# Gate and up products of 16 experts from two scaled fp16 parts in place of two fp32r parts

## The chip, the cores and the metric

The kernel runs on one NeuronCore of a Trainium2 chip (PE the matmul engine, DVE the vector engine, ACT the scalar engine, POOL, and SP for DMAs). The metric is the device time of one execution in microseconds.

## What is computed

A cross attention and then a soft mixture of experts on 16 batches of 100 tokens with 256 features. The expert part, with n tokens, 16 experts e of 64 slots s, and 512 hidden features f:

```python
logits = einsum('bnd,esd->bnes', x, se)
dispatch = softmax(logits, axis=1)
combine = softmax(logits.reshape(B, N, -1), axis=-1)
slots = einsum('bnd,bnes->besd', x, dispatch)
gate = gelu(einsum('besd,edf->besf', slots, Wg) + bg, approximate=False)
up = einsum('besd,edf->besf', slots, Wu) + bu
eout = einsum('besf,efo->beso', gate * up, Wd) + bd
out = x + einsum('bns,bso->bno', combine, eout)
```

Here x in the first line is a layer norm with gain norm_g and bias norm_b. Results are wanted at fp32 quality, so large products are made from a high and a low part of each operand: high x high, high x low and low x high.

## The kernel before

Three phases follow each other, each a block of its own, and at a block's end all engines meet.

**Attention** takes one batch per step of a hand-written table of slots. Its products of probabilities and values (L762) use fp16 probabilities as weights and 49 bf16 columns. In step 15 (B - 1) and the step before, DVE also prepares the first token norm of the next phase.

**Routing** runs steps t from -2 to 17. In step t, PE makes the logits of batch t + 1 (L1167), ACT copies those of batch t to l_sb (L1075), DVE takes maxima, ACT exponentiates (e_comb L1084, e_disp L1103, eight pieces), and for batch t - 1 DVE takes the reciprocal rz_slot (L1012), POOL scales (disp_n L964), PE transposes (L1138, L1152), and ACT and DVE copy the results out (combT L1091, dispT L1018) for SP to store in DRAM. The order on each engine is the order of the calls of `part`, with `part` of slot s + 6 for the batch before ahead of slot s. In routing's last steps, PE also makes the first slots of the expert phase (L1224). Gate and up weights of experts 0 and 1 (wgu) are loaded in steps -1 and 0.

**Experts** run as 8 pairs, `step(pair, first, last)`, of which six are a loop. Each pair has two halves h of the batches (8 batches x 64 slots = 512 columns) and two experts e; half and expert together are a unit. A unit is four chunks c of 128 hidden features, each with 6 gate and 6 up matmuls (L1539, 128 x 128 weights, 512 columns, two banks each in turn), and then the down product (L1579): 48 matmuls of 256 columns, whose order leaves chunk 3 for the 19th and later. After chunks 0 and 2 PE makes slots of the next half (mix L1512), after 1 and 3 it combines the half before (mix L1519). Per chunk ACT does the gelu (L1486), DVE (up + bias) x gate (L1430), ACT the high part hid_h (L1490) and DVE the low part hid_l (L1435). In a pair's first half, ACT and DVE also split the down weights (wd_h L1496 after chunk 1, wd_l L1441 after chunk 2). At a unit's end DVE adds the output bias in two parts (eo L1453, g = 0 and 1), each when PE has finished two of the four down tiles, and SP moves them to eo_pair (L1357).

The weights of the next pair are split in the second half: `weights_hi` on ACT (wgu_h, L1274) and `weights_lo` on DVE (wgu_l, L1279), expert 0's at the end of unit (h 1, e 0), expert 1's at the end of unit (h 1, e 1). For experts 0 and 1 this is done in routing, expert 0's in step 1, expert 1's in steps 15 and 16. At the start of each unit PE waits for them:

```python
pe.wait_ge(sl_ready, 4 * hs + 4)
pe.wait_ge(wl_ready[e], pair + 1)
```

## Time and profile before

| | |
|---|---|
| three runs | 1162.72, 1164.14 (median), 1166.11 us |
| the profiled execution | 1163.88 us, its span 1162.2 us |
| mean granted PE clock | 0.958 of 2.4 GHz |
| busy over the span | PE 91%, weight loads 75%, DVE 60%, ACT 50%, POOL 29% |
| phases in the span | attention to some 355 us, routing to 501, experts to the end |

All rows of the trace below are of the profiled execution, whose time is 1.7 us more than its span. Times in them are us from the span's start unless marked otherwise. A row's idle time in brackets is that of its engine just before the instruction, with what ended it.

### The profile page before, as it was taken

Reading aid. Unit: us, or ns where it says so; the run is one execution under the profiler, and the core shown is the slowest. Engines: PE = TensorE matmul, PEld = TensorE weight load, DVE = VectorE, ACT = ScalarE, POOL = GpSimd, SP = SyncE. Lnnn points to the kernel's source line nnn. Section 1 sums busy time; section 2 is a strip of 40 time slices with the busy share of each in tenths; the row PEclk is TensorE's granted clock in tenths of the full one; section 3 lists DMA queues with packets and bytes.
Section 4 is the critical chain, followed back from the end, with each engine's and each line's share of the span. In section 5 each row is a group of like instructions: output and inputs, shape, how many; then the busy total and the mean of one; then the engine's idle time right before and its main releaser. Section 6 shows DMA issues by size and latency. Waiting matters only on the chain.

```text
span 1162.2 us, 22171 instructions
## 1 busy us (share of the span) xinstructions
PE 1063.1 (91%) x7172; PEld 869.9 (75%) x7172; DVE 698.5 (60%) x1247; ACT 576.3 (50%) x1084; POOL 332.6 (29%) x348
## 2 busy tenths in 40 slices
PE   5688999999877888789999999999999999999997
PEld 3466777777663444478888888888888888888885
DVE  5556777777636888544555555655645555556544
ACT  2376878778655788733433343433424334333421
POOL 5267767667664343210010010100100100100000
PEclk8789999999958999889999999999999999999998
DMA  8858778678403534432142242432331331422123
GB/s 208 183 120 142 168 156 159 155 140 172 88 2 96 145 99 112 122 129 65 41 132 75 56 117 74 107 103 76 113 92 41 113 93 41 131 74 54 47 57 83
DMA packets 115080, 121.50 MB, mean 105 GB/s; under 512 B 46633, under 2 KB 105445, under 8 KB 115029
## 3 DMA queue, kind: packets, MB, share of 16 engines
q1 hardware_dynamic: 100908, 79.07, 30.5%
q0 software_dynamic: 10960, 40.67, 11.5%
q10 hardware_dynamic: 3160, 1.11, 0.6%
q8 instruction: 28, 0.46, 0.2%
q14 instruction: 24, 0.19, 0.1%
HBM read 73.87 MB, written 29.93 MB: 89 GB/s over the span
## 4 chain that ended last, share of the span: by engine, by line
PE 55%; DVE 1%; issue 1%; ACT 0%; DVEq 0%; ACTq 0%
PE down L1579 16%; PE gate L1539 15%; PE up L1539 15%; PE mix L1519 5%; PE mix L1512 4%; DVE gate_sb L1430 0%; ACT hid_h L1490 0%; DVE hid_l L1435 0%; DVE wd_l L1441 0%; DVE x L1415 0%; ACT gate_sb L1486 0%; DVE slot_l L1406 0%; DVEq L1633 0%; DVEq L1429 0%; DVEq L1412 0%
## 5 line engine op out<-in xcount | busy, mean ns | idle before, releaser
L1486 ACT ACTIVATE gate_sb<-gate,bgu 128x512 f32<-128x512 f32 x128 | 88.1, 689 | 222.3 <-PE gate L1539 207.7
L402 POOL TENSOR_TENSOR p_l<-p_f,p_h 121x800 f16<-121x800 f32 (+1 forms) x96 | 163.7, 1718 | 80.4 <-ACT p_h L652 79.5
L1490 ACT ACTIVATE hid_h<-gate_sb 128x512 fp32r<-128x512 f32 x128 | 80.9, 632 | 178.0 <-DVE gate_sb L1430 178.0
L1430 DVE SCALAR_TENSOR_TENSOR gate_sb<-up,bgu,gate_sb 128x512 f32<-128x512 f32 x128 | 95.9, 749 | 103.1 <-PE up L1539 101.3
L486 DVE TENSOR_REDUCE head_max<-at_rows 100x2 f32<-100x722 f32 x124 | 112.9, 910 | 71.8 <-PE at_rows L730 69.8
L1579 PE MATMUL down<-wd_h,hid_h 128*128 128x256 f32 x512 | 150.7, 294 | 0.7 <-DVE hid_l L1435 0.7
L1435 DVE TENSOR_TENSOR hid_l<-gate_sb,hid_h 128x512 fp32r<-128x512 f32 x128 | 88.6, 692 | 93.6 <-ACT hid_h L1490 93.6
L1579 PE MATMUL down<-wd_l,hid_h 128*128 128x256 f32 x512 | 144.8, 283 | 0.0
L1579 PE MATMUL down<-wd_h,hid_l 128*128 128x256 f32 x512 | 144.8, 283 | 0.0
L1263 POOL DMA_DIRECT2D wd<-in_Wd x16 | 12.2, 766 | 320.8 <-DVE eo L1453 300.4
L1579 PEld LDWEIGHTS down<-wd_h,hid_h 128*128 128x128 f32 x512 | 98.0, 191 | 3.4 <-issue 1.0
L1453 DVE TENSOR_TENSOR eo<-down,bd 128x512 f32<-128x512 f32 x64 | 44.3, 692 | 93.3 <-PE down L1579 93.3
L1579 PEld LDWEIGHTS down<-wd_l,hid_h 128*128 128x128 f32 x512 | 98.2, 192 | 0.8
L1579 PEld LDWEIGHTS down<-wd_h,hid_l 128*128 128x128 f32 x512 | 98.1, 192 | 0.0
L647 ACT ACTIVATE p_f<-at_cols 121x800 f32<-121x800 f32 (+1 forms) x96 | 79.7, 830 | 30.4 <-PE at_cols L742 29.4
L1539 PE MATMUL gate<-slot_h,wgu_h 128*128 128x512 f32 x256 | 91.0, 436 | 4.0 <-PEq L1631 4.0
L730 PE MATMUL at_rows<-kt,qt 100*100 100x362 f32 x248 | 74.5, 383 | 12.2 <-DVE head_max L486 11.4
L652 ACT ACTIVATE p_h<-p_f 121x800 f16<-121x800 f32 (+1 forms) x96 | 83.6, 871 | 3.0
L1539 PE MATMUL gate<-slot_l,wgu_h 128*128 128x512 f32 x256 | 80.7, 397 | 0.0
L1539 PE MATMUL up<-slot_l,wgu_h 128*128 128x512 f32 x256 | 80.1, 394 | 0.0
L742 PE MATMUL at_cols<-qt,kt 104*121 104x200 f32 (+1 forms) x384 | 67.8, 303 | 13.4 <-DMA qt<-max_p 8.8
L1539 PE MATMUL up<-slot_h,wgu_h 128*128 128x512 f32 x256 | 80.0, 394 | 0.0
(165 smaller groups left out, 2279.1 us busy)
## 6 DMA issues: line engine op xcount, KB each, us to landing
eo_pair<-eo SPq DMA_DIRECT2D x128, 128.0 KB, 2.4
k_parts<-kq_n SPq DMA_DIRECT2D x16, 724.0 KB, 3.7
kt<-k_parts SPq DMA_DIRECT2D x32, 362.0 KB
wgu<-in_Wg POOLq DMA_DIRECT2D x16, 512.0 KB, 6.2
wgu<-in_Wu POOLq DMA_DIRECT2D x16, 512.0 KB, 6.9
wd<-in_Wd POOLq DMA_DIRECT2D x16, 512.0 KB, 5.2
combine<-combT SPq DMA_DIRECT2D x16, 400.0 KB, 4.0
dispatch<-dispT SPq DMA_DIRECT2D x16, 400.0 KB
```

The source lines that it names most:

```text
L402: nc.gpsimd.tensor_tensor(p_l[i][0:kn, :, 0:N], p_f[i][0:kn], p_h[i][0:kn, :, 0:N], ALU.subtract).then_inc(p_low, 1)
L486: nc.vector.tensor_reduce(head_max[:, :, r], bank[0:N, :, 0:S], AX.X, ALU.max).then_inc(max_ready, 1)
L647: nc.scalar.activation(p_f[u][0:kn].rearrange("k (g e) n -> k g (e n)", g=2), cols_ps[0:kn, :, 0:4 * N], ACT.Exp, scale=1.0 / SCALE_INV).t ...
L652: nc.scalar.activation(p_h[u][0:kn, :, 0:N], p_f[u][0:kn], ACT.Copy).then_inc(p_hi, 1)
L730: mm = nc.tensor.matmul(bank[0:N, c, 0:SW], q[0:ROWS_A, r, N * c:N * c + N], k[0:ROWS_A, r, :], start=True, stop=True)
L742: mm = nc.tensor.matmul(cols_ps[0:kn, e // 2, (e % 2) * 2 * N:(e % 2 + 1) * 2 * N], kt[t % NBUF][0:ROWS_B, r, j * KC:j * KC + kn], qt[t % ...
L1430: nc.vector.scalar_tensor_tensor(gate[c % 2][:], up_ps[c % 2][:], bu_col(bgu, pair, e, c), gate[c % 2][:], ALU.add, ALU.mult).then_inc(hid ...
L1435: nc.vector.tensor_tensor(hid_l[:, c, :], gate[c % 2][:], hid_h[:, c, :].bitcast(F32), ALU.subtract).then_inc(hidl_ready, 1)
L1486: nc.scalar.activation(gate[c % 2][:], gate_ps[c % 2][:], ACT.Gelu, bias=bg_col(bgu, pair, e, c)).then_inc(gelu_ready, 1)
L1490: nc.scalar.activation(hid_h[:, c, :], gate[c % 2][:], ACT.Copy).then_inc(hidh_ready, 1)
L1539: mm = nc.tensor.matmul(bank[:], wt[e][:, kc, i, c * P:(c + 1) * P], st[h][:, kc, e, :, :].rearrange("p b s -> p (b s)"), start=(k == 0), ...
L1579: mm = nc.tensor.matmul(down_ps[t // 2][:, t % 2, :], ht[:, c, t * P:(t + 1) * P], wt[:, c, :], start=(c == 0 and k == 0), stop=(c == FC - ...
```

## The change

The parts of the gate and up weights and of the slots become fp16, two parts each, three products as before. So that they fit fp16's range, both sides are scaled by powers of two: the norm's gain and bias by s_x, from the largest values of gain and bias (`norm_scaled`, on DVE at the end of attention's step 14), and each expert's gate and up weights by a factor from its largest absolute weight. That maximum is reduced per partition on DVE (`max_gate_up`), sent through DRAM by SP so that every partition has all 128 (`share_maxima`), and turned into scales by eight DVE instructions (`expert_scales`). The scales are taken out again in instructions that exist already: the copy to l_sb, the gelu, hid_h and hid_l, the last of which becomes a scalar_tensor_tensor, as does weights_lo. The down product stays fp32r.

The steps are placed so: for pair 0, the maxima at the end of routing steps 1 and 2, `share_maxima` at the start of step 13, the scales at the end of step 14, `weights_hi` of expert 0 ahead of l_sb in step 15 and `weights_lo` of expert 0 at the end of step 15. For the next pair: the maxima in unit (h 0, e 1), one ahead of each eo; `share_maxima` behind unit (h 1, e 0); the scales in unit (h 1, e 1) after chunk 2; both `weights_hi` at the end of that unit, and `weights_lo` of expert 0 and 1 behind its eo of g = 0 and 1. Several semaphores of attention are merged into one, with the counts waited for adapted.

```diff
+            nc.vector.tensor_reduce(mg, keep["norm_g"][:], AX.X, ALU.max, apply_absolute_value=True).then_inc(slot_step, 1)
+            nc.vector.tensor_reduce(mb, keep["norm_b"][:], AX.X, ALU.max, apply_absolute_value=True).then_inc(slot_step, 1)
...
+            nc.vector.scalar_tensor_tensor(norm, mg, SMALLEST, mb, ALU.max, ALU.add).then_inc(slot_step, 1)
...
+            nc.vector.tensor_tensor(power.bitcast(I32), norm.bitcast(I32), bits, ALU.bitwise_and).then_inc(slot_step, 1)
...
+            nc.vector.tensor_tensor(over.bitcast(I32), power.bitcast(I32), bits, ALU.bitwise_xor).then_inc(slot_step, 1)
...
+            nc.vector.tensor_scalar(s_x, over, 2.0 ** (FP16_TOP - 6), None, ALU.mult).then_inc(slot_step, 1)
+            nc.vector.tensor_scalar(inv_x, power, 2.0 ** (5 - FP16_TOP), None, ALU.mult).then_inc(slot_step, 1)
+            nc.vector.tensor_scalar(n256, norm, 256.0, None, ALU.mult).then_inc(slot_step, 1)
+            dve.wait_ge(slot_step, 3 * SC + 9)
+            for n in ("norm_g", "norm_b"):
+                nc.vector.tensor_scalar(keep[n][:], keep[n][:], s_x, None, ALU.mult).then_inc(slot_step, 1)
...
+            if t == B - 3:
+                share_maxima(sp, keep, 0)
...
-            if t == 1:
+            if t in (1, 2):
+                max_gate_up(nc, dve, keep, t - 1, 0)
+            if t == B - 4:
+                dve.wait_ge(keep["bias_in"], 32)
+            if t == B - 2:
+                expert_scales(nc, dve, keep, 0)
+            if t == B - 1:
                 weights_lo(nc, dve, keep, 0, 0)
...
+                if t == B - 1:
+                    weights_hi(nc, act, keep, 0, 0)
+                nc.scalar.activation(l_sb[:], logits[0:N, :, :].rearrange("p a b -> p (a b)"), ACT.Copy,
+                                     scale=keep["norm_top"][0:N, 6:7]).then_inc(lcopy_ready, 1)
...
-            if t == 1:
-                weights_hi(nc, act, keep, 0, 0)
...
-        "wgu_h": [sb(f"wgu_h{e}", [P, 2, 2, F], F32R) for e in range(2)],
-        "wgu_l": [sb(f"wgu_l{e}", [P, 2, 2, F], F32R) for e in range(2)],
+        "wgu_h": [sb(f"wgu_h{e}", [P, 2, 2, F], F16) for e in range(2)],
+        "wgu_l": [sb(f"wgu_l{e}", [P, 2, 2, F], F16) for e in range(2)],
...
-        "slot_h": [sb(f"slot_h{i}", [P, 2, 2, BH, SL], F32R) for i in range(2)],
-        "slot_l": [sb(f"slot_l{i}", [P, 2, 2, BH, SL], F32R) for i in range(2)],
+        "slot_h": [sb(f"slot_h{i}", [P, 2, 2, BH, SL], F16) for i in range(2)],
+        "slot_l": [sb(f"slot_l{i}", [P, 2, 2, BH, SL], F16) for i in range(2)],
...
+def max_gate_up(nc, dve, keep, e, pair):
+
+    dve.wait_ge(keep["wgu_in"][e], 32 * pair + 32)
+    if not (isinstance(pair, int) and pair == 0):
+        dve.wait_ge(keep["max_moved"], 32 * pair)
+    dve.sem_inc(keep["waited"], 1)
+    nc.vector.tensor_reduce(keep["maxima"][:, 0, e:e + 1], keep["wgu"][e][:].rearrange("p c i f -> p (c i f)"), AX.X, ALU.max,
+                            apply_absolute_value=True).then_inc(keep["max_ready"], 1)
...
+def share_maxima(eng, keep, pair):
...
+    eng.wait_ge(keep["max_ready"], MAXIMA * pair + MAXIMA)
...
+        eng.wait_ge(keep["scale_step"], SCALE_STEPS * pair)
...
+    eng.dma_start(flat.rearrange("(p j) -> p j", p=P), keep["maxima"][:].rearrange("p k e -> p (k e)")).then_inc(keep["max_moved"], 16)
+    eng.wait_ge(keep["max_moved"], 32 * pair + 16)
+    eng.sem_inc(keep["waited"], 1)
+    eng.dma_start(keep["all_maxima"][:], flat.partition_broadcast(P)).then_inc(keep["max_moved"], 16)
...
+def expert_scales(nc, dve, keep, pair):
...
+    def done(n):
+        dve.wait_ge(step, SCALE_STEPS * pair + n)
+        dve.sem_inc(keep["waited"], 1)
+
+    dve.wait_ge(keep["max_moved"], 32 * pair + 32)
+    if not (isinstance(pair, int) and pair == 0):
+        done(0)
+    nc.vector.tensor_reduce(top[:, 0, :], keep["all_maxima"][:].rearrange("q (p j) -> q j p", p=P), AX.X, ALU.max).then_inc(step, 1)
+    done(1)
+    nc.vector.tensor_scalar(top[:, 1, :], top[:, 0, :], SMALLEST, None, ALU.max).then_inc(step, 1)
+    done(2)
+    nc.vector.tensor_tensor(top[:, 2, :].bitcast(I32), top[:, 1, :].bitcast(I32), bits[:, 0:2], ALU.bitwise_and).then_inc(step, 1)
+    done(3)
+    nc.vector.tensor_tensor(top[:, 3, :].bitcast(I32), top[:, 2, :].bitcast(I32), bits[:, 0:2], ALU.bitwise_xor).then_inc(step, 1)
+    done(4)
+    nc.vector.tensor_scalar(keep["w_scale"][:, bass.ds(pair, 1), 0, :].rearrange("p o e -> p (o e)"), top[:, 3, :], 2.0 ** (FP16_TOP - 2), None, ALU.mult).then_inc(step, 1)
+    nc.vector.tensor_scalar(un_gate, top[:, 2, :], 2.0 ** (1 - FP16_TOP), inv_x, ALU.mult, ALU.mult).then_inc(step, 1)
+    done(6)
+    for e in range(2):
+        nc.vector.tensor_scalar(keep["bu_s"][:, bass.ds(2 * pair + e, 1), :].rearrange("p o c -> p (o c)"),
+                                keep["bgu"][:, 1, bass.ds(2 * pair + e, 1), :].rearrange("p o c -> p (o c)"),
+                                keep["w_scale"][:, bass.ds(pair, 1), 0, e], s_x, ALU.mult, ALU.mult).then_inc(step, 1)
...
 def weights_hi(nc, act, keep, e, pair):
     act.wait_ge(keep["wgu_in"][e], 32 * pair + 32)
-    nc.scalar.activation(keep["wgu_h"][e][:], keep["wgu"][e][:], ACT.Copy).then_inc(keep["wh_ready"][e], 1)
+    act.wait_ge(keep["scale_step"], SCALE_STEPS * pair + SCALE_STEPS)
+    act.sem_inc(keep["waited"], 1)
+    nc.scalar.activation(keep["wgu_h"][e][:], keep["wgu"][e][:], ACT.Copy, scale=keep["w_scale"][:, bass.ds(pair, 1), 0, e]).then_inc(keep["wh_ready"][e], 1)
 
 
 def weights_lo(nc, dve, keep, e, pair):
     dve.wait_ge(keep["wh_ready"][e], pair + 1)
-    nc.vector.tensor_tensor(keep["wgu_l"][e][:], keep["wgu"][e][:], keep["wgu_h"][e][:].bitcast(F32), ALU.subtract).then_inc(keep["wl_ready"][e], 1)
+    dve.sem_inc(keep["waited"], 1)
+    nc.vector.scalar_tensor_tensor(keep["wgu_l"][e][:], keep["wgu"][e][:], keep["w_scale"][:, bass.ds(pair, 1), 0, e], keep["wgu_h"][e][:],
+                                   ALU.mult, ALU.subtract).then_inc(keep["wl_ready"][e], 1)
...
+                    if h == 1 and e == 0 and not last:
+                        share_maxima(sp, keep, pair + 1)
...
-                        nc.vector.scalar_tensor_tensor(gate[c % 2][:], up_ps[c % 2][:], bu_col(bgu, pair, e, c), gate[c % 2][:],
+                        nc.vector.scalar_tensor_tensor(gate[c % 2][:], up_ps[c % 2][:], keep["bu_s"][:, bass.ds(2 * pair + e, 1), c], gate[c % 2][:],
                                                        ALU.add, ALU.mult).then_inc(hid_ready, 1)
...
-                        nc.vector.tensor_tensor(hid_l[:, c, :], gate[c % 2][:], hid_h[:, c, :].bitcast(F32), ALU.subtract).then_inc(hidl_ready, 1)
+                        nc.vector.scalar_tensor_tensor(hid_l[:, c, :], gate[c % 2][:], keep["un_gate"][:, bass.ds(2 * pair + e, 1)], hid_h[:, c, :].bitcast(F32),
+                                                       ALU.mult, ALU.subtract).then_inc(hidl_ready, 1)
...
+                        if h == 1 and e == 1 and c == 2 and not last:
+                            expert_scales(nc, dve, keep, pair + 1)
                     for g in range(2):
+                        if h == 0 and e == 1 and not last:
+                            max_gate_up(nc, dve, keep, g, pair + 1)
                         dve.wait_ge(down_done, 2 * u + g + 1)
                         if not (first and h == 0):
                             dve.wait_ge(eo_moved[1 - h][e][g], 32 * pair + 32 * h)
                         dve.wait_ge(wd_in[e], 32 * pair + 32)
...
-                    if h == 1 and not last:
-                        weights_lo(nc, dve, keep, e, pair + 1)
+                        if h == 1 and e == 1 and not last:
+                            weights_lo(nc, dve, keep, g, pair + 1)
...
+                        nc.scalar.activation(gate[c % 2][:], gate_ps[c % 2][:], ACT.Gelu, bias=bg_col(bgu, pair, e, c),
+                                             scale=keep["un_gate"][:, bass.ds(2 * pair + e, 1)]).then_inc(gelu_ready, 1)
                         act.wait_ge(hid_ready, FC * u + c + 1)
...
+                        nc.scalar.activation(hid_h[:, c, :], gate[c % 2][:], ACT.Copy,
+                                             scale=keep["un_gate"][:, bass.ds(2 * pair + e, 1)]).then_inc(hidh_ready, 1)
                         if h == 0 and c == 1:
...
-                    if h == 1 and not last:
-                        act.wait_ge(up_done, FC * u + FC)
-                        weights_hi(nc, act, keep, e, pair + 1)
+                    if h == 1 and e == 1 and not last:
+                        for x in range(2):
+                            act.wait_ge(up_done, FC * (u - 1 + x) + FC)
+                            weights_hi(nc, act, keep, x, pair + 1)
```

How the order moves, at two places. First the DVE queue over the last chunks of a pair's last unit and its end (`top`, `w_scale`, `un_gate`, `bu_s` are the scales, `x` is the combined output, `eo` the output with bias). Before:

```order
L1406 TENSOR_TENSOR slot_l<-mix,slot_h 128x4x2x64 [waits sh_ready,slots_done]
L1430 SCALAR_TENSOR_TENSOR gate_sb<-up,bgu,gate_sb 128x512 [waits gelu_ready,up_done]
L1435 TENSOR_TENSOR hid_l<-gate_sb,hid_h 128x512 [waits down_done,hidh_ready]
L1415 SCALAR_TENSOR_TENSOR x<-mix,rz,x 100x256 [waits acc_ready,comb_done]
L1415 SCALAR_TENSOR_TENSOR x<-mix,rz,x 100x256
L1453 TENSOR_TENSOR eo<-down,bd 128x512 [waits wd_in1,eo_moved010,down_done]
L1453 TENSOR_TENSOR eo<-down,bd 128x512 [waits wd_in1,eo_moved011,down_done]
L1279 TENSOR_TENSOR wgu_l<-wgu,wgu_h 128x2048 [waits wh_ready1]
```

After, from chunk 2 on, and then the unit's end:

```order
L1513 TENSOR_TENSOR slot_l<-mix,slot_h 128x4x2x64 [waits sh_ready,slots_done]
L1356 TENSOR_REDUCE top<-all_maxima 128x2 [waits wmax_moved,scale_step]
L1358 TENSOR_SCALAR top<-top 128x2 [waits scale_step]
L1360 TENSOR_TENSOR top<-top,exponent 128x2 [waits scale_step]
L1362 TENSOR_TENSOR top<-top,exponent 128x2 [waits scale_step]
L1364 TENSOR_SCALAR w_scale<-top 128x2 [waits scale_step]
L1365 TENSOR_SCALAR un_gate<-top,norm_top 128x2
L1368 TENSOR_SCALAR bu_s<-bgu,w_scale,norm_top 128x4 [waits scale_step]
L1368 TENSOR_SCALAR bu_s<-bgu,w_scale,norm_top 128x4
L1537 SCALAR_TENSOR_TENSOR gate_sb<-up,bu_s,gate_sb 128x512 [waits gelu_ready,up_done]
L1542 SCALAR_TENSOR_TENSOR hid_l<-gate_sb,un_gate,hid_h 128x512 [waits down_done,hidh_ready]
```

```order
L1522 SCALAR_TENSOR_TENSOR x<-mix,rz,x 100x256
L1565 TENSOR_TENSOR eo<-down,bd 128x512 [waits wd_in1,eo_moved010,down_done]
L1383 SCALAR_TENSOR_TENSOR wgu_l<-wgu,w_scale,wgu_h 128x2048 [waits wh_ready0]
L1565 TENSOR_TENSOR eo<-down,bd 128x512 [waits wd_in1,eo_moved011,down_done]
L1383 SCALAR_TENSOR_TENSOR wgu_l<-wgu,w_scale,wgu_h 128x2048 [waits wh_ready1]
```

The scales stand ahead of chunk 3's gate_sb and hid_l, and both wgu_l stand here, where expert 0's stood one unit earlier.

Second the DVE queue at the end of routing, steps 14 and 15, and the ACT queue in step 15. Before, DVE, then ACT:

```order
L1018 COPY dispT<-rt_out 100x512 [waits disp_stored,dispT_done] x2
L1012 RECIPROCAL rz_slot<-z_slot 128x8 [waits dispn_ready,edisp_ready]
L1002 TENSOR_REDUCE neg_max<-l_sb 100x1 [waits ecomb_ready,lcopy_ready]
L1007 RECIPROCAL rz<-z_tok 100x1 [waits ecomb_ready]
L1024 TENSOR_REDUCE neg_max_s<-rt_lT 128x4 [waits edisp_ready,lT_done] x2
L1018 COPY dispT<-rt_out 100x512 [waits disp_stored,dispT_done] x2
L1240 TENSOR_TENSOR slot_l<-rt_slots,slot_h 128x4x2x64 [waits sh_ready]
L1240 TENSOR_TENSOR slot_l<-rt_logits,slot_h 128x4x2x64 [waits sh_ready]
```

```order
L1075 ACTIVATE l_sb<-rt_logits 100x1024 [waits tokmax_ready,ecomb_ready,lT_done,logits_done]
L1274 ACTIVATE wgu_h<-wgu 128x2048 [waits wgu_in1]
L1091 ACTIVATE combT<-rt_out 128x400 [waits comb_stored,combT_done] x2
L1232 ACTIVATE slot_h<-rt_slots 128x4x2x64 [waits slots_done]
L1232 ACTIVATE slot_h<-rt_logits 128x4x2x64 [waits slots_done]
L1084 ACTIVATE e_comb,z_tok<-l_sb,neg_max 100x1024 [waits rz_ready,combT_done,tokmax_ready]
```

After, DVE in two pieces, then ACT:

```order
L1049 COPY dispT<-rt_out 100x512 [waits disp_stored,dispT_done] x2
L1356 TENSOR_REDUCE top<-all_maxima 128x2 [waits wmax_moved]
L1358 TENSOR_SCALAR top<-top 128x2 [waits scale_step]
L1360 TENSOR_TENSOR top<-top,exponent 128x2 [waits scale_step]
L1362 TENSOR_TENSOR top<-top,exponent 128x2 [waits scale_step]
L1364 TENSOR_SCALAR w_scale<-top 128x2 [waits scale_step]
```

```order
L1055 TENSOR_REDUCE neg_max_s<-rt_lT 128x4 [waits edisp_ready,lT_done] x2
L1049 COPY dispT<-rt_out 100x512 [waits disp_stored,dispT_done] x2
L1383 SCALAR_TENSOR_TENSOR wgu_l<-wgu,w_scale,wgu_h 128x2048 [waits wh_ready0]
L1285 TENSOR_TENSOR slot_l<-rt_slots,slot_h 128x4x2x64 [waits sh_ready]
L1285 TENSOR_TENSOR slot_l<-rt_logits,slot_h 128x4x2x64 [waits sh_ready]
L1043 RECIPROCAL rz_slot<-z_slot 128x8 [waits dispn_ready,edisp_ready]
```

```order
L1377 ACTIVATE wgu_h<-wgu,w_scale 128x2048 [waits wgu_in0,ecomb_ready,scale_step,tokmax_ready,logits_done,lT_done]
L1114 ACTIVATE l_sb<-rt_logits,norm_top 100x1024
L1377 ACTIVATE wgu_h<-wgu,w_scale 128x2048 [waits wgu_in1,scale_step]
L1131 ACTIVATE combT<-rt_out 128x400 [waits comb_stored,combT_done] x2
L1277 ACTIVATE slot_h<-rt_slots 128x4x2x64 [waits slots_done]
L1277 ACTIVATE slot_h<-rt_logits 128x4x2x64 [waits slots_done]
```

The scales come between dispT and rz_slot of step 15, expert 0's wgu_l between dispT and slot_l, and expert 0's wgu_h ahead of l_sb.

## Rows read from the trace of the kernel before

**Rows 1.** The page, part 4: the chain that ended last, share of the span by line.

```profile
PE down L1579 16%; PE gate L1539 15%; PE up L1539 15%; PE mix L1519 5%; PE mix L1512 4%; DVE gate_sb L1430 0%; ACT hid_h L1490 0%; DVE hid_l L1435 0%; DVE wd_l L1441 0%; DVE x L1415 0%; ACT gate_sb L1486 0%; DVE slot_l L1406 0%; DVEq L1633 
```

**Rows 2.** Windows: us, busy us (instructions) of PE, PEld, DVE, ACT, POOL, clock, DMA share, GB/s.

```profile
664.90:746.10 81.20, 81.20 (x482) 71.43 (x481) 46.11 (x68) 30.45 (x44) 7.10 (x11) 1.00 0.33 88
```

**Rows 3.** Timeline, PE, one unit: start us, us, engine, line, what [idle before <- releaser].

```profile
699.89 0.28 PE L1579 MATMUL down<-wd_l,hid_h 128*128 128x256 f32 x1
...
705.41 0.28 PE L1579 MATMUL down<-wd_h,hid_l 128*128 128x256 f32 x1
...
706.00 0.62 PE L1539 MATMUL gate<-slot_l,wgu_h 128*128 128x512 f32 x2
...
708.28 1.05 PE L1512 MATMUL mix<-disp,xn 100*128 100x128 f32 x8
```

**Rows 4.** Timeline, PE, attention: first and last of fourteen fp16 matmuls.

```profile
204.49 0.18 PE L762 MATMUL at_out<-v,p_l 121*128 121x49 bf16 x1
...
204.84 0.18 PE L762 MATMUL at_out<-v,p_l 121*128 121x49 bf16 x1
```

**Rows 5.** Timeline, ACT, DVE and PE where one pair ends and the next begins.

```profile
659.79 1.90 ACT L1274 ACTIVATE wgu_h<-wgu 128x2048 fp32r<-128x2048 f32 x1
...
663.64 0.69 DVE L1453 TENSOR_TENSOR eo<-down,bd 128x512 f32<-128x512 f32 x1 [2.25 <-PE down L1579]
...
665.69 2.28 DVE L1279 TENSOR_TENSOR wgu_l<-wgu,wgu_h 128x2048 fp32r<-128x2048 f32 x1
...
664.88 0.63 PE L1539 MATMUL gate<-slot_h,wgu_h 128*128 128x512 f32 x2
```

**Rows 6.** Timeline, DVE and PE, first unit of the expert phase.

```profile
519.05 0.69 DVE L1435 TENSOR_TENSOR hid_l<-gate_sb,hid_h 128x512 fp32r<-128x512 f32 x1 [0.70 <-ACT hid_h L1490]
...
519.89 0.35 PE L1579 MATMUL down<-wd_h,hid_h 128*128 128x256 f32 x1 [0.32 <-DVE hid_l L1435]
```

**Rows 7.** Timeline, DVE, routing: small instructions.

```profile
456.42 0.19 DVE L1012 RECIPROCAL rz_slot<-z_slot 128x8 f32<-128x8 f32 x1
...
456.53 0.37 DVE L1027 BATCH_NORM_STATS2 rt_st<-x 100x6 f32<-100x256 f32 x1
...
459.60 0.43 DVE L1035 BATCH_NORM_STATS2 rt_st<-rt_y 100x6 f32<-100x256 f32 x1
...
460.17 0.18 DVE L1038 BATCH_NORM_AGGREGATE rt_mv<-rt_st 100x2 f32<-100x6 f32 x1
```

**Rows 8.** Timeline, DVE and PE, last unit of a pair.

```profile
658.47 0.75 DVE L1430 SCALAR_TENSOR_TENSOR gate_sb<-up,bgu,gate_sb 128x512 f32<-128x512 f32 x1 [0.92 <-PE up L1539]
...
659.92 0.69 DVE L1435 TENSOR_TENSOR hid_l<-gate_sb,hid_h 128x512 fp32r<-128x512 f32 x1 [0.70 <-ACT hid_h L1490]
...
659.25 0.28 PE L1579 MATMUL down<-wd_l,hid_h 128*128 128x256 f32 x1
```

**Rows 9.** Timeline, DVE, a unit of the first half.

```profile
700.81 0.69 DVE L1435 TENSOR_TENSOR hid_l<-gate_sb,hid_h 128x512 fp32r<-128x512 f32 x1 [0.70 <-ACT hid_h L1490]
```

**Rows 10.** Timeline, ACT, DVE and PE, end of routing.

```profile
481.37 1.07 ACT L1075 ACTIVATE l_sb<-rt_logits 100x1024 f32<-100x1024 f32 x1
...
481.61 1.29 DVE L1018 COPY dispT<-rt_out 100x512 f32<-100x512 f32 x2 [3.31 <-PE rt_out L1152]
...
490.22 0.20 DVE L1012 RECIPROCAL rz_slot<-z_slot 128x8 f32<-128x8 f32 x1 [0.63 <-ACT e_disp L1103]
...
501.37 1.19 PE L1539 MATMUL gate<-slot_h,wgu_h 128*128 128x512 f32 x2 [4.03 <-PEq L1631]
```

**Rows 11.** Timeline, DVE, attention, step 15.

```profile
338.58 0.56 DVE L518 TENSOR_REDUCE o_sum<-at_out 100x128 f32<-100x384 f32 x1 [5.15 <-PE at_out L762]
```

**Rows 12.** Timeline, PE, routing: idle stretches and logits matmuls.

```profile
379.46 3.68 PE L1167 MATMUL rt_logits<-seT,rt_xnT 128*100 128x512 f32 x8
...
468.21 6.12 PE L1167 MATMUL rt_logits<-seT,rt_xnT 128*100 128x512 f32 x8 [2.94 <-ACT rt_xnT L1112]
...
487.95 1.13 PE L1138 MATMUL rt_out<-ident,e_comb 100*128 100x100 f32 x8 [1.25 <-DVE dispT L1018]
```

116 lines of the change are left out of this document (73 added, 43 removed).

## The prediction

> **What bounds the kernel now.** I read the chain that ended last first: its five largest shares are PE's lines of the expert phase, down 16%, gate and up 15% each, the two mix products 5% and 4%; every DVE or ACT line rounds to nothing [rows 1]. Next the windows, one pair of experts at a time: in the 81.2 us from 664.9 to 746.1 PE is busy for all of it at full clock, with DVE at 46.1 and ACT at 30.4 [rows 2]. So from 501 us on a nanosecond off a matmul counts in full, and DVE and ACT work is free as long as it ends before PE asks for it. The third view is therefore the timeline, for each place where the change puts DVE or ACT work ahead of something PE wants. Before 501 us (attention, routing) PE, DVE and ACT wait for each other in turn, and no engine is a cover by itself.
>
> **Gate and up matmuls.** There are 8 pairs x 2 halves x 2 experts x 4 chunks x 12 = 1,536. Ten of them start between 706.00 and 708.28, 228 ns each [rows 3]; 512 columns at the full 2.4 GHz level are 213 ns, so 15 ns are not columns. The down matmuls, 256 columns of the same type, start every 120 ns (5.52 us for 46), 13 above their 107 [rows 3]. fp16 weights show in attention only: 14 matmuls of 49 columns, each with its own weight load, take 0.35 us, 25 ns each, 5 above their 20 [rows 4]. So fp16 gives at least 213 and at most 218 ns. I take 216, nearer the fp16 row: 12 ns x 1,536 = **-18.4** (bounds -15 and -23). A unit (one expert, one half) falls from 20.3 to 19.7 us, a pair by 2.3.
>
> **End of a pair.** Both wgu_l subtractions now stand after the pair's last unit, expert 0's between the two eo additions; PE needs expert 0's before its next matmul. Today that one was done a whole unit earlier. The first eo addition runs from 663.64 to 664.33, and a DVE instruction can start 0.08 before its predecessor's end (456.42 + 0.19 against 456.53), so the subtraction starts at 664.25, takes 2.28 (now at 665.69) and ends at 666.53; PE could go on at 664.88 [rows 5, 7]. With 0.15 us from DVE's end to PE's start (519.05 + 0.69 against 519.89 [rows 6]) that is a gap of 1.8 us, 7 times: **+12.6** (bounds 1.6 and 2.1 each). ACT's two casts (1.90 each, from 659.79 [rows 5]) are done for expert 0 at 661.7 and are covered. The second subtraction ends near 669.4, just when the first up product is ready, and is covered; a later DVE would delay gate_sb, which has two chunks of spare.
>
> **The scales.** Eight DVE instructions stand at chunk 2 of the pair's last unit, seven between pairs. Independent small ones start 0.11 apart (456.42, 456.53), one that waits for its predecessor 0.57 after a start of 0.43 length, so 0.14 after its end [rows 7]. With 0.18 for a small one and 0.41 for the reduction over 256: 0.55 + 3 x 0.32 + 0.11 + 0.32 + 0.11 + 0.11 = 2.2 us (bounds 1.1, all independent, and 4.6, all at 0.57). DVE idles 0.92 there before gate_sb at 658.47 [rows 8]; chunk 3 comes 0.14 sooner and the longer hid_l and one more ACT wait take 0.1, so 0.68 are left and gate_sb slips 1.5. hid_l ends at 660.61, PE's first matmul that reads it (the 18th after 659.25, 0.12 apart) would start at 661.29 [rows 8]: 0.53 of spare with the 0.15, less 0.1. The down product stalls 1.05 us, **+7.3** (bounds 0 and 15). The Trainium skill, "VectorE: DVE Perf Modes", section "The DRAIN you can't avoid", says that a semaphore after each of eight copies cost nothing extra, so a chain would run like independent instructions. By it the chain is 1.1 us, this term 0, and the whole some 9 us less. The 0.57 against 0.11 in this trace speaks against it, and I go by the trace.
>
> **Other units.** hid_l becomes a three-operand instruction (gate_sb, also one, takes 0.75 against 0.69 [rows 8]). In the first half DVE is already the later one at chunk 3 (wd_l): hid_l ends at 701.50, PE wants it at 699.89 + 17 x 0.12 = 701.93 [rows 3, 9]. The 0.28 of spare lose 0.14 to PE and 0.2 to the two chains: 0.1 us x 16 = **+1.6** (0 to 4).
>
> **The maxima.** Two reductions of 2,048 (about 2.28, like the subtraction [rows 5]) stand in the last unit of the first half, one in front of each eo addition. DVE waits 2.25 us for PE in front of the first eo addition [rows 5], so it fits; the second ends about when the next up product does. The two small DMAs through DRAM stand behind the eo_pair stores on SP, which has nothing else for 20 us; some 5 us for both against 12 until the scales are wanted. Nothing.
>
> **Routing.** Early: one subtraction (2.28) and its ACT cast leave step 1, two reductions come at steps 1 and 2. DVE gains some 0.5 us and loses 2.2: **+1.7** (0 to 3). Tail: the scales stand behind the dispT copies of 481.61 [rows 10], so they run from 482.8 to 484.9. ACT's cast of expert 0 now stands ahead of l_sb and waits for them: l_sb at 486.7 where it was 481.37 [rows 10], **+5.3**, and all of ACT's exponentials follow it. DVE has the subtraction of expert 0 ahead of rz_slot, which was at 490.22 when ACT had just delivered [rows 10]; it would be ready at 495.5 and runs at 496.5, one more: **+6.3** in all (bounds 4 and 9). The last slot products and the phase change behind them, with the first expert matmul at 501.37 [rows 10], move along. The ten instructions on the norm's bound and gains in attention's step 14 are some 2.5 us by the same small rows; they fall just before a stretch of 5.15 us in which DVE waits for PE, up to 338.58 [rows 11]: nothing, and 2.5 without that cover.
>
> **The clock.** The new gap of 1.8 us lies between one of 1.25, after which the clock stayed at the 2.4 GHz level, and one of 2.94, after which eight logits matmuls took 6.12 in place of 3.68 at the 1.2 GHz level [rows 12]. A fall costs up to 2.4. None in seven is 0, seven 17; I take one and a half, **+3.6**.
>
> **The sum.** -18.4 + 12.6 + 7.3 + 1.6 + 1.7 + 6.3 + 3.6 = +14.7. The profiled execution took 1163.88 us, 0.3 under the median of the runs, so 1178.6. A measurement of this kernel tells 0.3%, 3.5 us, from no change.
>
> **Rivals.**
> *DVE's chains are cheap.* If the scales take 1.1 us they hide at chunk 2, the tail gains 1.1, and with a clock that holds: -18.4 + 12.6 + 1.6 + 1.7 + 5.2 = +2.7, **1166.6**. For it: independent small ones start 0.11 apart. Against: each of these waits. 14%.
> *The clock falls at every boundary.* 7 x 2.4 for 3.6: **1192**. For it: routing shows falls after gaps not much longer. Against: PE is dense on both sides of this one. 14%.
> *No gain on PE.* The 15 ns belong to the stream and not to the type; then the losses stand alone, **1197**. For it: down shows nearly the same surplus at half the columns. Against: the fp16 rows' 5. 5%.
> *Faster: fp16 matmuls that start sooner than their columns last.* The place is the 1,536 matmuls; the losses are 33 us, so it decides from a pace under 204 ns (24 x 1,536 = 37, with 3.5 for the measurement). At 131 ns it would be 97 x 1,536 = 149 less, **1048**. Nothing in the trace runs under one column per cycle. The page "TensorE: Matmul & The Clock Gate", section "Back-to-back issue gap", of the Trainium skill gives 131 ns for load and matmul pairs of 512 columns; by it the result would be that. With it I count a world where every loss is at its lower bound. 5%.
>
> **Chances and range.** The forecast keeps 62%. Faster by more than 0.3%: 5%; within: the first rival less its slower half and some of the forecast's low side, 11%; slower: 84%. The range reaches from the cheap chains (1165) to a clock that falls each time (1192).
>
> **What would show it.** Right: gate and up pace near 216 ns; PE idle about 1.8 us before the first gate matmul of seven pairs, ended by DVE wgu_l, and some 1 us inside down, ended by hid_l; first expert matmul near 509; a loop pair about 82 us against 81.3. Wrong: a pace of 228, scales in 1 us, an idle PE that waits for a DMA or for max_moved, or a phase change before 505.

## The result, and the profile after

Four runs of the changed kernel gave 1191.48 to 1200.52 us, median 1196.57, against 1164.39 before: ratio 1.0274 (95% interval 1.0225 to 1.0322). It is 32 us slower; 1178.6 with a range up to 1192 was forecast. The profiled execution took 1199.46 us, its span 1197.7.

Three numbers cut the added 35.5 us of span: routing starts (first rt_x matmul) at 358.97 us where it was 356.13, the first expert matmul is at 514.57 (before 501.37 [rows 10]), and the span ends 683.1 us after it (before 660.8). So attention gives +2.8, routing +10.4 and the experts +22.3.

The page of the changed kernel, part 4, the chain that ended last, by engine and (the start of the line) by line, answers to [rows 1]:

```profile
PE 44%; DVE 4%; DMA 4%; issue 2%; ACT 1%; SPq 1%; DVEq 0%; ACTq 0%
PE down L1695 13%; PE gate L1655 11%; PE up L1655 11%; PE mix L1635 4%; PE mix L1628 4%; DMA weight_maxima<-maxima 2%; DMA all_maxima<-weight_maxima 1%; DVE wgu_l L1383 1%; DVE gate_sb L1537 1%; ACT hid_h L1604 1%; SPq L1462 1%; DVE hid_l L1542 1%; DMA disp<-dispatch 0%; DVE eo L1565 0%; DVE top L1356 0%
```

and its waits of PE:

```profile
PE down L1695 <- DVE hid_l L1542: 16.4, 9, 3.1
...
PE gate L1655 <- DVE wgu_l L1383: 10.8, 6, 1.8
```

Where DVE and ACT lines rounded to nothing, DVE and two DMAs of the maxima now stand on the chain. PE waits for hid_l and wgu_l at the ends of the pairs. The timeline shows the pace of the gate and up matmuls, rows of two (to be read with [rows 3]):

```profile
521.29 0.60 PE L1655 MATMUL gate<-slot_h,wgu_h 128*128 128x512 f16 x2
...
525.61 0.59 PE L1655 MATMUL up<-slot_l,wgu_h 128*128 128x512 f16 x2
```

Ten rows of two later is 4.32 us: 216 ns a matmul, as taken. Now the end of the second pair (SP's two DMAs and POOL's load, DVE, PE), which answers to [rows 5, 8]:

```profile
663.60 0.33 SPq L1335 DMA_DIRECT2D weight_maxima<-maxima  x1
...
669.49 0.32 SPq L1338 DMA_DIRECT2D all_maxima<-weight_maxima  x1
...
662.13 0.77 POOL L1308 DMA_DIRECT2D wd<-in_Wd  x1 [25.87 <-DVE eo L1565]
...
673.96 0.42 DVE L1356 TENSOR_REDUCE top<-all_maxima 128x2 f32<-128x256 f32 x1 [0.66 <-DMA all_maxima<-weight_maxima]
...
674.53 0.17 DVE L1358 TENSOR_SCALAR top<-top 128x2 f32<-128x2 f32 x1 [0.16 <-DVE top L1356]
...
675.57 0.17 DVE L1364 TENSOR_SCALAR w_scale<-top 128x2 f32 x1 [0.25 <-DVE top L1362]
...
676.22 0.60 DVE L1368 TENSOR_SCALAR bu_s<-bgu,w_scale,norm_top  x2 [0.29 <-DVE un_gate L1365]
...
676.73 0.75 DVE L1537 SCALAR_TENSOR_TENSOR gate_sb<-up,bu_s,gate_sb 128x512 f32<-128x512 f32 x1
...
678.38 0.75 DVE L1542 SCALAR_TENSOR_TENSOR hid_l<-gate_sb,un_gate,hid_h 128x512 fp32r<-128x512 f32 x1 [0.90 <-ACT hid_h L1604]
...
682.31 2.34 DVE L1383 SCALAR_TENSOR_TENSOR wgu_l<-wgu,w_scale,wgu_h 128x2048 f16<-128x2048 f32 x1
...
676.56 0.28 PE L1695 MATMUL down<-wd_h,hid_l 128*128 128x256 f32 x1
...
679.28 0.36 PE L1695 MATMUL down<-wd_h,hid_h 128*128 128x256 f32 x1 [2.44 <-DVE hid_l L1542]
...
684.90 0.59 PE L1655 MATMUL gate<-slot_h,wgu_h 128*128 128x512 f16 x2 [1.81 <-DVE wgu_l L1383]
```

The gap ahead of the first gate matmul is 1.81 us, as forecast. The one inside down is not: 2.44 us here, in the seven pairs 1.47, 2.44, 1.69, 2.11, 2.48, 3.08 and 1.95, where 1.05 was taken for each. Two things are in it. DVE can start on all_maxima at 673.96, 10.4 us after the first of its two DMAs, where some 5 were taken, and waits 0.66 for it; and the scales take 2.77 us (673.96 to gate_sb at 676.73) and not 2.2. Where the scales do not stand, DVE's idle time ahead of chunk 3's gate_sb is 0.58, close to the 0.68 I had left:

```profile
654.14 0.75 DVE L1537 SCALAR_TENSOR_TENSOR gate_sb<-up,bu_s,gate_sb 128x512 f32<-128x512 f32 x1 [0.58 <-PE up L1655]
```


The clock fell to its lower level behind two of the seven gaps: windows behind those of 2.48 and 1.95 us, and last one behind the gap of 3.08, PE alone (us, busy, PEclk, DMA share, GB/s):

```profile
931.20:933.90 2.70, 2.69 (x12) 0.50 0.00 0
...
1101.20:1104.40 3.20, 3.15 (x15) 0.51 0.00 0
...
1017.50:1020.50 3.00, 3.00 (x26) 1.00 0.00 0
```

Each last unit is as long as its gap inside down and 21.9 us, within 0.05, except these two. The one of the 2.48 gap is 1.3 longer; that of the 1.95 gap, the last of the seven, is 1.5 longer than the same unit of e5 beside its gap (a last unit that ends with a gap of 1.67 and not 1.81). That is 2.8 us for the clock.

### The profile page after: what moved, and what is told of

Same layout as the page of the kernel before. It is cut to its first block, busy times and chain, and to the rows that moved or that the text cites. A ratio compares the mean times of both kernels' runs of the same rounds, so it can differ in the third digit from the quotient of the medians.

```text
span 1197.7 us, 22529 instructions
## 1 busy us (share of the span) xinstructions
PE 1055.0 (88%) x7172; PEld 740.9 (62%) x7172; DVE 756.7 (63%) x1337; ACT 600.6 (50%) x1084; POOL 333.0 (28%) x349
## 3 DMA queue, kind: packets, MB, share of 16 engines
q1 hardware_dynamic: 103280, 80.19, 30.8%
## 4 chain that ended last, share of the span: by engine, by line
PE 44%; DVE 4%; DMA 4%; issue 2%; ACT 1%; SPq 1%; DVEq 0%; ACTq 0%
PE down L1695 13%; PE gate L1655 11%; PE up L1655 11%; PE mix L1635 4%; PE mix L1628 4%; DMA weight_maxima<-maxima 2%; DMA all_maxima<-weight_maxima 1%; DVE wgu_l L1383 1%; DVE gate_sb L1537 1%; ACT hid_h L1604 1%; SPq L1462 1%; DVE hid_l L1542 1%; DMA disp<-dispatch 0%; DVE eo L1565 0%; DVE top L1356 0%
## 5 line engine op out<-in xcount | busy, mean ns | idle before, releaser
L1598 ACT ACTIVATE gate_sb<-gate,bgu,un_gate 128x512 f32<-128x512 f32 x128 | 99.2, 775 | 211.2 <-PE gate L1655 201.4
L1604 ACT ACTIVATE hid_h<-gate_sb,un_gate 128x512 fp32r<-128x512 f32 x128 | 92.4, 722 | 188.7 <-DVE gate_sb L1537 188.7
L1542 DVE SCALAR_TENSOR_TENSOR hid_l<-gate_sb,un_gate,hid_h 128x512 fp32r<-128x512 f32 x128 | 96.2, 752 | 120.5 <-ACT hid_h L1604 120.5
L1695 PE MATMUL down<-wd_h,hid_h 128*128 128x256 f32 x512 | 153.6, 300 | 18.9 <-DVE hid_l L1542 16.4
L1537 DVE SCALAR_TENSOR_TENSOR gate_sb<-up,bu_s,gate_sb 128x512 f32<-128x512 f32 x128 | 95.9, 750 | 67.0 <-PE up L1655 59.6
L1655 PE MATMUL gate<-slot_h,wgu_h 128*128 128x512 f16 x256 | 76.9, 382 | 16.6 <-DVE wgu_l L1383 10.8
L1655 PE MATMUL gate<-slot_h,wgu_l 128*128 128x512 f16 x256 | 76.6, 381 | 0.0
L1655 PE MATMUL gate<-slot_l,wgu_h 128*128 128x512 f16 x256 | 76.5, 381 | 0.0
L1655 PE MATMUL up<-slot_h,wgu_h 128*128 128x512 f16 x256 | 76.4, 380 | 0.0
```

What stands on the lines that cost most here:

```text
L1537: nc.vector.scalar_tensor_tensor(gate[c % 2][:], up_ps[c % 2][:], keep["bu_s"][:, bass.ds(2 * pair + e, 1), c], gate[c % 2][:], ALU.add, A ...
L1542: nc.vector.scalar_tensor_tensor(hid_l[:, c, :], gate[c % 2][:], keep["un_gate"][:, bass.ds(2 * pair + e, 1)], hid_h[:, c, :].bitcast(F32) ...
L1598: nc.scalar.activation(gate[c % 2][:], gate_ps[c % 2][:], ACT.Gelu, bias=bg_col(bgu, pair, e, c), scale=keep["un_gate"][:, bass.ds(2 * pai ...
L1604: nc.scalar.activation(hid_h[:, c, :], gate[c % 2][:], ACT.Copy, scale=keep["un_gate"][:, bass.ds(2 * pair + e, 1)]).then_inc(hidh_ready, 1)
L1655: mm = nc.tensor.matmul(bank[:], wt[e][:, kc, i, c * P:(c + 1) * P], st[h][:, kc, e, :, :].rearrange("p b s -> p (b s)"), start=(k == 0), ...
L1695: mm = nc.tensor.matmul(down_ps[t // 2][:, t % 2, :], ht[:, c, t * P:(t + 1) * P], wt[:, c, :], start=(c == 0 and k == 0), stop=(c == FC - ...
```

## The experiments

Times of the kernels run together are compared with their own runs of before. To keep run-to-run changes of attention out (its end lay between 353.9 and 359.0 us in the profiles of these kernels, 354.06 in e3 with the changed kernel's attention code), the text goes by unit lengths, from a unit's first gate matmul to the next unit's, and by the length of routing, from the first rt_x to the first gate matmul (before 145.24, changed 155.60).

**e1: the type alone.** The four wgu and slot tiles become F16 in the kernel before, which leaves out the scaling.

```diff
-        "wgu_h": [sb(f"wgu_h{e}", [P, 2, 2, F], F32R) for e in range(2)],
+        "wgu_h": [sb(f"wgu_h{e}", [P, 2, 2, F], F16) for e in range(2)],
...
```

> The kernel before with its gate/up weight parts and slot parts as fp16, no scales, no maxima and nothing moved; it leaves out the scaling. Theory: in the changed kernel a unit without a stall (h 1, e 0) takes 19.73 us where it took 20.33, so the type alone is worth 0.6 us x 32 units = 19 us, and everything else in the change is loss: time near 1145, pace of gate and up 216 ns, no PE idle at the ends of pairs. Rival: the shorter units are partly an effect of the placement (the DMA load or DVE work being elsewhere), and fp16 with its work in the old places makes PE wait for DVE in the first halves: time 1150 to 1156.

1144.26 us (ratio 0.9837, 0.9806 to 0.9867), every unit of the loop 19.64 us (before 20.33), the loop pair 78.56. The type is worth 0.69 us a unit, 21 us in all, and needs no other placement.

```profile
661.11 0.61 PE L1539 MATMUL gate<-slot_h,wgu_h 128*128 128x512 f16 x2
...
739.67 0.60 PE L1539 MATMUL gate<-slot_h,wgu_h 128*128 128x512 f16 x2
```

**e2: the order alone**, in fp32r.

```diff
-                    if h == 1 and not last:
-                        weights_lo(nc, dve, keep, e, pair + 1)
+                        if h == 1 and e == 1 and not last:
+                            weights_lo(nc, dve, keep, g, pair + 1)
...
```

> The kernel before, still fp32r, with only the order changed: both weights_hi and both weights_lo at the end of unit (h 1, e 1), expert 0's subtraction between the two eo additions. Theory: the gap before the first gate matmul of a pair is DVE's order alone and as long as in the changed kernel, 1.8 us x 7 = 12.6: time near 1177, clock unchanged, nothing inside down. Rival: the gap in the changed kernel is there because hid_l and eo come late behind the scales; then PE waits under 1 us here and the time is below 1171.

1178.36 us (1.0132, 1.0102 to 1.0163), +13.1. The gap is the order's own. Behind the first of the seven the clock was at its 1.2 GHz level for some 3 us, and that unit is 1.6 us longer than the same one of the next pairs (21.98, 20.42); behind the other six it stayed up:

```profile
668.33 0.70 PE L1540 MATMUL gate<-slot_h,wgu_h 128*128 128x512 f32 x2 [1.75 <-DVE wgu_l L1279]
```

**e3: the pair's chain a unit earlier.**

```diff
-                    if h == 1 and e == 0 and not last:
+                    if h == 0 and e == 1 and not last:
                         share_maxima(sp, keep, pair + 1)
...
-                        if h == 1 and e == 1 and c == 2 and not last:
+                        if h == 1 and e == 0 and c == 3 and not last:
                             expert_scales(nc, dve, keep, pair + 1)
...
-                        if h == 1 and e == 1 and not last:
-                            weights_lo(nc, dve, keep, g, pair + 1)
+                    if h == 1 and not last:
+                        weights_lo(nc, dve, keep, e, pair + 1)
...
```

> The changed kernel with the pair's chain one unit earlier: share_maxima behind (h 0, e 1), the scales in (h 1, e 0) behind chunk 3's work and ahead of eo, weights_hi and weights_lo of each expert at the end of its own second-half unit as before the change. Theory: the three losses at a pair's end (hid_l 15.2 us in seven, wgu_l 12.5, clock some 3.5) all go and nothing takes their place, since DVE idles 1.8 to 2.2 us ahead of eo: last units 19.8 us, loop pair 79.8 to 80.0, time 1163 to 1168 (29 to 33 less than the changed kernel). Rival: the 10 us of the two DMAs now end too late for the scales, so that eo and expert 0's subtraction slip into (h 1, e 1) and PE waits there: time 1172 to 1185.

1168.55 us (1.0046, 1.0012 to 1.0079), 28 less than the changed kernel. All gaps at the pair's end are gone; the loop pair takes 80.65 where up to 80.0 was expected. What is left over sits in the last unit (20.68): weights_hi now waits for the scales, wgu_l for it, and the late x holds PE's next slots.

```profile
652.96 2.35 DVE L1383 SCALAR_TENSOR_TENSOR wgu_l<-wgu,w_scale,wgu_h 128x2048 f16<-128x2048 f32 x1 [1.02 <-ACT wgu_h L1377]
...
661.53 1.16 PE L1627 MATMUL mix<-disp,xn 100*128 100x128 f32 x8 [0.78 <-DVE x L1522]
```

**e5: only the two DMAs a unit earlier** (the first edit of e3).

> The changed kernel with share_maxima of a pair behind (h 0, e 1) in place of (h 1, e 0); the scales stay where they are, behind chunk 2 of (h 1, e 1). Theory: of the stall inside down, the part that DVE spent waiting for all_maxima (0.66, 0.36, 0.71, 1.31, 0.18 us, 3.2 in seven pairs) goes and with it the clock falls behind it (3.5); the chain itself stays, so each pair still stalls 1.5 to 1.7 us at hid_l: time 1189 to 1193. Rival: the DMAs set the whole stall, and it falls under 0.5 us a pair: time below 1185.

1189.48 us (1.0217, 1.0186 to 1.0247). DVE no longer waits for all_maxima, the clock stays up through all eight pairs, and the last units of the loop are 23.6 us; the stall stays at 1.65 to 1.69 (1.46 in the first pair). So the chain of eight instructions is the larger part and the DMAs the smaller. The first DMA also got faster, 1 KB in 3.0 us, up to the issue of the second, where it took 5.9: here the next load of down weights starts 17 us later (743.08), there it had started 1.5 us before (662.13 above).

```profile
726.02 0.33 SPq L1335 DMA_DIRECT2D weight_maxima<-maxima  x1
...
729.02 0.32 SPq L1338 DMA_DIRECT2D all_maxima<-weight_maxima  x1
...
759.47 0.36 PE L1695 MATMUL down<-wd_h,hid_h 128*128 128x256 f32 x1 [1.68 <-DVE hid_l L1542]
```

**e4: routing's share_maxima cut in two**, the write at the end of step 2, the read at the start of step 12.

> The changed kernel with routing's share_maxima cut in two: the write to DRAM at the end of step 2, the read at the start of step 12, so that SP waits for neither. Scales, casts and subtractions stay. Theory: SP stood 5.8 us behind its own write, and the combine and dispatch stores behind it, so combT waited (1.8 us) and all of steps 14 and 15 came later: the first expert matmul comes 1.5 to 2.5 us sooner than in the changed kernel. Rival: the tail hangs on the scales alone, and the store's delay is hidden: no difference over 0.5 us at the first expert matmul.

1197.76 us (1.0287, 1.0264 to 1.0311), routing 156.54: no gain, 0.9 longer. The gain of 1.5 to 2.5 did not come: the blocked SP was not what held the tail, as the rival says. The 0.9 are no effect of the edit in the main: the first combT, ahead of the steps that it touches, is already 0.7 later (14.5 us into routing, in the changed kernel 13.8). Routing with the changed kernel's code took 155.1 to 155.6 in four profiles.

**e6: e4, and the first scales and expert 0's split in steps 13 and 14.**

```diff
+            if s == AT_RT["dispT_out"][0] and t == B - 3:
+                expert_scales(nc, dve, keep, 0)
+            if s == AT_RT["dispT_out"][0] and t == B - 2:
+                weights_lo(nc, dve, keep, 0, 0)
...
-                if t == B - 1:
+                if t == B - 2:
                     weights_hi(nc, act, keep, 0, 0)
...
```

> e4 and beside it the scales in step 13 ahead of dispT (DVE idled 4.5 us there before the change), weights_hi of expert 0 ahead of l_sb in step 14, weights_lo of expert 0 ahead of dispT in step 14 (3.3 us idle). Theory: of the 13.2 us by which the experts start later than before the change, 3.2 arise in attention and 1.6 in steps 1 and 2; the other 8.4 are the scales and expert 0's split in the tail and the blocked SP, and nearly all go: first expert matmul some 7.5 us sooner than in the changed kernel, time near 1189. Rival: step 13 and 14 have no more room, since the chain there goes over ACT; gain under 3 us.

1193.12 us (1.0263, 1.0233 to 1.0293), routing 149.03, 6.6 less. The median of the runs shows only about half of that; its interval is 7 us wide, and the pairs' stalls, 1.5 to 2.6 us here, vary from run to run. So the placement in the tail costs 6.6 in the profile, and 3.8 are left, 1.6 of them from steps 1 and 2 (combT of step 13 comes 112.57 us into routing in the changed kernel, before 110.99; in e3 and e5, which have the same routing, 112.0). With e6's placement routing took 146.5 to 149.2 us in six profiles (e6 and e8 to e12), so the 6.6 is good to about 1 to 2 us.

**e7: the down weights' split one chunk earlier.**

> The changed kernel with the split of the down weights one chunk earlier in the first half: wd_h behind chunk 0, wd_l behind chunk 1. Theory: first-half units take 20.12 us where the second half's undisturbed one takes 19.73, because wd_l and slot_l stand ahead of chunk 3's gate_sb and hid_l on DVE; with wd_l a chunk earlier they fall to 19.75, 6 us in 16 units: time near 1190.5. Rival: the 0.39 us are the longer hid_l and ACT's chain, which chunk 3 has in any unit, or wd_l now delays chunk 2: units stay above 20.0.

1211.49 us (1.0415, 1.0391 to 1.0439): 15 slower than the changed kernel. First-half units of the loop take 21.5. wd_l now stands ahead of x, and PE's next slots need the PSUM bank that x frees:

```profile
606.30 1.22 DVE L1549 TENSOR_TENSOR wd_l<-wd,wd_h 128x1024 fp32r<-128x1024 f32 x1
...
607.44 0.87 DVE L1522 SCALAR_TENSOR_TENSOR x<-mix,rz,x 100x256 f32<-100x256 f32 x2
...
608.36 0.82 PE L1628 MATMUL mix<-disp,xn 100*128 100x128 f32 x5 [1.61 <-DVE x L1522]
```

**e8: e3, e6 and e7 together.**

> e3, e6 and e7 together. Theory: the losses are separate and add up; what is left of the change is 19 us on PE, less 1.6 in steps 1 and 2 of routing and under 2 elsewhere: time near 1147 to 1151, below both kernels, loop pair 79.0. Rival: with the pair's chain in (h 1, e 0) and wd_l earlier DVE becomes the late one somewhere, and the sum of gains falls short by 5 us or more: 1155 to 1160.

1184.33 us (1.0192, 1.0164 to 1.0220). Both the theory (1147 to 1151) and the rival (to 1160) missed it by far. It carries e7's loss, as e9 shows; the loop pairs are 83.5 to 85.2. PE waits 1.73 us for x in the first units of the first and of the last three loop pairs alike, but only in the first three did the clock stand at its 1.2 GHz level for some 3 us behind it (594.9 to 598.3 us in the first), which is their 1.7 us. That led to three more.

**e9: e3 and e6 without e7.**

> e3 and e6 together, the down split left where the change has it. Theory: the loss of e8 against e3 is the down split alone, and the placement in the pairs and in routing add up: loop pair 80.65 as in e3, routing 149.0 as in e6, time 1168.6 - 6.1 = near 1162, no more than 0.3% from before. Rival: the earlier work in routing's steps 13 and 14 is given back at the change of phase: above 1166.

1163.5 us (0.9989, 0.9973 to 1.0005): no difference from before, the loop pair 80.64. The two placements add up.

**e10: maxima and DMAs in unit (h 0, e 0), scales at the end of (h 0, e 1).**

```diff
-                    if h == 0 and e == 1 and not last:
+                    if h == 0 and e == 0 and not last:
                         share_maxima(sp, keep, pair + 1)
...
-                        if h == 0 and e == 1 and not last:
+                        if h == 0 and e == 0 and not last:
                             max_gate_up(nc, dve, keep, g, pair + 1)
...
+                    if h == 0 and e == 1 and not last:
+                        expert_scales(nc, dve, keep, pair + 1)
...
```

> e9 with the pair's maxima in unit (h 0, e 0), its share_maxima behind that unit and the scales at the end of unit (h 0, e 1). Theory: in e3 the last unit is 20.68 us and not 19.73, since weights_hi of expert 0 waits for the scales (1.02 us of DVE idle ahead of wgu_l) and DVE reaches gate_sb and the combined output x late (PE waits 0.78); with the scales ready a unit earlier that goes, 0.95 x 6 = 6 us: time near 1156. Rival: the gate and up weights of the next pair have not landed at the end of unit (h 0, e 0), so that the maxima hold up eo and the next unit: first-half units above 20.4, time above 1162.

1159.71 us (0.9968, 0.9954 to 0.9982): 0.3% faster than the kernel before, and much faster than the changed one, with the whole computation. 1156 was expected. The last unit is 19.73; the loop pair is 80.08, not 79.7, since (h 1, e 0) now takes 20.11 behind the scales.

**e11: wd_l behind chunk 1's x.**

> e10 with wd_h behind chunk 0 on ACT and wd_l behind chunk 1's combined output on DVE (in e7 it stood ahead of it, and PE's next slots waited 1.6 us for that output, whose PSUM bank they take). Theory: the place behind x frees PE from that wait, and what is left of the first half's 0.39 us goes: first-half units 19.7 to 19.9, time 1150 to 1153. Rival: DVE has not 1.2 us to spare in chunks 1 and 2 together, gate_sb of chunk 2 comes late, and units stay at or above 20.1.

1162.21 us (0.9982, 0.9966 to 0.9999), 2.5 more than e10, first-half units 20.48 and 20.33. PE still waits 0.59 and 0.45 us for x: the rival held, DVE has no room there.

**e12: e10 without the scale in hid_h and hid_l.**

```diff
-                        act.sem_inc(waited, 1)
-                        nc.scalar.activation(hid_h[:, c, :], gate[c % 2][:], ACT.Copy,
-                                             scale=keep["un_gate"][:, bass.ds(2 * pair + e, 1)]).then_inc(hidh_ready, 1)
+                        nc.scalar.activation(hid_h[:, c, :], gate[c % 2][:], ACT.Copy).then_inc(hidh_ready, 1)
...
-                        nc.vector.scalar_tensor_tensor(hid_l[:, c, :], gate[c % 2][:], keep["un_gate"][:, bass.ds(2 * pair + e, 1)], hid_h[:, c, :].bitcast(F32),
-                                                       ALU.mult, ALU.subtract).then_inc(hidl_ready, 1)
+                        nc.vector.tensor_tensor(hid_l[:, c, :], gate[c % 2][:], hid_h[:, c, :].bitcast(F32), ALU.subtract).then_inc(hidl_ready, 1)
```

> e10 with hid_h as a plain copy without scale and without its extra semaphore instruction, and hid_l as the two-operand subtraction again; it leaves out the division of the hidden features by the scales, so its output is scaled. Theory: the first half's 20.12 us against e1's 19.64 are the chain gate_sb, hid_h, hid_l of chunk 3: on ACT a scale read from memory makes hid_h 0.09 us longer (722 ns against 632), the three-operand hid_l 0.06 (752 against 692), and the wait ahead of hid_l grew from 0.70 to 0.90; with these gone the first-half units fall to 19.7 to 19.8, some 5 to 6 us in all: time near 1154. Rival: the time is lost in wd_l and slot_l ahead of that chain, which stay: units stay at 20.0 or more, time above 1157.

1149.85 us (0.9888, 0.9851 to 0.9926), 10 less than e10, twice what was expected. First-half units fall to 19.63, which is e1's unit, (h 1, e 1) falls from 19.73 to 19.63, and (h 1, e 0) from 20.11 to 19.70. So what the change adds to the two instructions that "exist already" costs 10 us in e10. The edit takes out two things at once on ACT, the scale and a semaphore instruction ahead of hid_h, and it does not part them. The gelu keeps its scale, and with it e12 still has e1's unit: there it costs nothing. The groups by line, ACT and DVE, of the changed kernel in the experts' stretch (busy, mean ns, idle before):

```profile
L1604 ACT ACTIVATE hid_h<-gate_sb,un_gate 128x512 fp32r<-128x512 f32 x128 | 92.4, 722 | 188.7 <-DVE gate_sb L1537 188.7
...
L1542 DVE SCALAR_TENSOR_TENSOR hid_l<-gate_sb,un_gate,hid_h 128x512 fp32r<-128x512 f32 x128 | 96.2, 752 | 120.5 <-ACT hid_h L1604 120.5
```

and the same two of the kernel before:

```profile
L1490 ACT ACTIVATE hid_h<-gate_sb 128x512 fp32r<-128x512 f32 x128 | 80.9, 632 | 178.0 <-DVE gate_sb L1430 178.0
...
L1435 DVE TENSOR_TENSOR hid_l<-gate_sb,hid_h 128x512 fp32r<-128x512 f32 x128 | 88.6, 692 | 93.6 <-ACT hid_h L1490 93.6
```

hid_h got 90 ns longer, hid_l 60, and DVE's wait for hid_h rose from 93.6 to 120.5 us in 128 (0.2 each). The other 0.12 of it is hid_h's start, 0.15 us behind the end of gate_sb (695.50 to 695.65) where it was 0.03 (757.30 to 757.33).

## Why the prediction was wrong, term by term

The direction, the pace and the gap at a pair's end came as forecast; the sum was 18 us short, outside the range. Two terms failed most, the scales with the maxima and the other units. The sizes, measured:

| term | forecast | measured | from |
|---|---|---|---|
| gate and up | -18.4 | -21 | e1 |
| end of a pair | +12.6 | +13.1 | e2 |
| scales, with the maxima | +7.3 | +17.0 | e5, below |
| other units | +1.6 | +8.5 | unit lengths against e1, below |
| routing, early and tail | +8.0 | +10.4 | profile, e6 |
| clock | +3.6 | +2.8 | below |
| sum | +14.7 | +30.8 | medians +32.2 |

The terms come from different kernels, so their sum can't be exact. The profiled execution is 32.7 us longer without attention's 2.8; 0.85 of the missing 1.9 lie in the very first unit of the expert phase (23.03 us, before 22.18), which varied from 21.3 to 23.2 between the profiles of these kernels.

- **Gate and up.** Right in mechanism, 2.6 us small in size. e1's unit is 0.69 shorter, and 48 x 12 ns make 0.58. The rest is in the pace before: the ten matmuls read at 706.00 stand 228 ns apart, but the twelve of a whole chunk, from 664.88 [rows 5] to the mix product behind them, take 2.76 us, 230 each, and 14 x 48 ns are 0.67:

```profile
667.64 0.61 PE L1512 MATMUL mix<-disp,xn 100*128 100x128 f32 x4
```

Two rivals fell with it. "No gain on PE" had 1197 as its time, and that this is the measured median is chance: its pace of 228 was not there. The other goes by the sub-column pace: the Trainium skill's 131 ns ("TensorE: Matmul & The Clock Gate", "Back-to-back issue gap") is not met by any row, 216 is, 3 above its columns.
- **End of a pair.** Right by mechanism and by size, a gap of 1.8 us seven times.
- **The scales: the step that failed first.** The mechanism and the place (hid_l, at the 18th matmul of down) were right, the price was not. e5, in which nothing waits for a DMA and the clock stays up, has last units of 23.6; 19.73 is the unit without any of it and e2's end of a pair 1.9. So the chain costs 1.97 us x 7 = 13.8 where 1.05 each was taken, inside the bounds (0 to 15), and DVE's waits for all_maxima another 3.2. Of the 0.9 that was missing, 0.57 is the chain: in routing, where addresses are constants, the same eight took 2.34 us (487.42 to 489.76), in the loop 2.77, with gaps of 0.25 and 0.29 where 0.14 was taken (by the row, 0.57 less 0.43). The stall follows the chain: in the first pair, which stands outside the loop, the chain took 2.55 us and the gap inside down is 1.47, in the next but one 2.77 and 1.69. The rest is slack counted too high: 0.10 ahead of gate_sb (0.58 for 0.68), and 0.16 from gate_sb to the end of hid_l, a stretch that got 0.26 longer (wait and hid_l, as above) where 0.1 was taken. Some 0.1 stays open.
- **The maxima: "nothing" was wrong.** I gave both DMAs some 5 us from the eo_pair stores; they took 9.4 to 11. The write stands right behind unit (h 1, e 0), where POOL starts the load of the down weights, and took 5.7 to 6.6 us in that company, 2.9 to 3.3 without (e5); even there both took 7. DVE waited for them in five of the seven pairs, 3.2 us in all; e5, without these waits, had no clock fall in its pairs either.
- **Other units: the second step that failed.** I took 0.1 us in sixteen first-half units, with 4 us as the upper bound. Against e1, those of the changed kernel are 0.48 longer in the loop and the second half's 0.1, 8.5 us in all without the phase's very first unit. e12 against e10 shows that the cause is what was added to hid_h and hid_l; its 10 us are more, since some 2.3 of them lie in unit (h 1, e 0), 20.11 in e10 and 19.73 in the changed kernel. The place was right, the price was not: I took 0.2 for what the chains of chunks 2 and 3 gain together. From chunk 2's gate_sb, the last for which DVE waits for PE, to the end of chunk 3's hid_l it was 5.92 us, and is 6.46. Before and after:

```profile
756.55 0.75 DVE L1430 SCALAR_TENSOR_TENSOR gate_sb<-up,bgu,gate_sb 128x512 f32<-128x512 f32 x1 [0.72 <-PE up L1539]
...
761.78 0.69 DVE L1435 TENSOR_TENSOR hid_l<-gate_sb,hid_h 128x512 fp32r<-128x512 f32 x1 [0.70 <-ACT hid_h L1490]
```

```profile
694.75 0.75 DVE L1537 SCALAR_TENSOR_TENSOR gate_sb<-up,bu_s,gate_sb 128x512 f32<-128x512 f32 x1 [0.27 <-PE up L1655]
...
700.46 0.75 DVE L1542 SCALAR_TENSOR_TENSOR hid_l<-gate_sb,un_gate,hid_h 128x512 fp32r<-128x512 f32 x1 [0.91 <-ACT hid_h L1604]
```

That is 0.27 a chunk, the 0.2 of longer wait and the 0.06 of hid_l. Since wd_l and slot_l fill the time between the two chunks, both gains arrive at the last hid_l: 0.54, less the 0.14 of spare that the faster PE left, is 0.40 of the 0.48. I had left out that ACT's hid_h would itself become longer and start later.
- **Routing.** Early 1.6 for 1.7 (1.0 in e3 and e5). The tail is 8.8 for 6.3, near the upper bound of 9. e6 takes 6.6 back. That l_sb hangs on the scales was right (ACT waits 3.93 for bu_s). Counted from the start of routing, l_sb comes 7.8 us later, with the early 1.6 in it: 6.2 for the 5.3 forecast. I had let e_comb follow at the old distance, but it comes 9.4 later, since ACT now waits 1.43 for PE's slot product in between:

```profile
490.07 2.00 ACT L1377 ACTIVATE wgu_h<-wgu,w_scale 128x2048 f16<-128x2048 f32 x1 [3.93 <-DVE bu_s L1368]
...
491.98 1.10 ACT L1114 ACTIVATE l_sb<-rt_logits,norm_top 100x1024 f32<-100x1024 f32 x1
...
497.18 0.60 ACT L1277 ACTIVATE slot_h<-rt_slots 128x512 f16<-128x512 f32 x1 [1.43 <-PE rt_slots L1269]
```

- **The clock.** Near in size and in part by luck: two falls of 1.4 us where one and a half of 2.4 were taken. Both came behind gaps inside down, none behind the 1.8 us at a pair's end; in e2 one of the seven such gaps had a fall behind it. The rival in which it falls at every boundary is out.
- **Attention.** The ten instructions on the norm's bound were covered, as said; the 2.8 us of the profiled execution are run-to-run (e3, with the same attention code, starts routing at 354.06, earlier than before the change).
- **The cheap-chain rival** rested on small instructions 0.11 us apart. What the Trainium skill measured on eight copies, that a semaphore after each cost nothing extra ("VectorE: DVE Perf Modes", "The DRAIN you can't avoid"), would have hidden the scales if it held for such chains; in this trace it does not. Small instructions that each wait for the one before start 0.31 to 0.32 us apart, with 0.16 to 0.17 of their own time (e5):

```profile
755.06 0.16 DVE L1360 TENSOR_TENSOR top<-top,exponent 128x2 int32<-128x2 int32 x1 [0.15 <-DVE top L1358]
...
755.37 0.16 DVE L1362 TENSOR_TENSOR top<-top,exponent 128x2 int32<-128x2 int32 x1
```

## What to carry to other kernels

Where PE is busy throughout, a cheaper matmul pays in full, but only if the preparation it needs is ready a unit ahead: the same computation cost 32 us with its preparation late and gained 4 with it early (e10). Before calling a scale "folded into an instruction that exists", look whether that instruction stands in a chain which the bound engine waits for, and add up what the chain gains over all the chunks since its engine last waited for the bound one. Give a small DMA the time that it takes beside the transfers that start with it, not that of a quiet moment.

## What the runs showed of the hardware

- A 1 KB write of 128 pieces from SBUF to DRAM, up to the issue of the next DMA, took 2.9 to 3.3 us in e5 and 5.7 to 6.6 us right behind the start of a 512 KB load; in routing, right behind the start of a 400 KB store, it took 6.3. The 128 KB eo_pair stores land in 2.4 (median).
- An activation whose scale comes from memory took 722 ns where the plain copy took 632, and the gelu 775 where it took 689, at 128 x 512.
- Eight small DVE instructions, most of which wait for the one before, took 2.34 us in routing and 2.33 in e3's first pair, where the addresses are constants, and 2.77 in e3's loop pairs, at the same place with addresses from the loop's register.
- The clock did not fall by the length of the gap alone: behind gaps of 1.95 and 2.48 us inside down (1.79 in e4) it was at the 1.2 GHz level for some 3 us, behind those of 2.44 and 3.08 it stayed at 2.4 GHz. In e2 it fell behind one of seven gaps of 1.6 to 1.75 at pair ends, in e8 behind three of six waits of 1.73. In e5's pairs, with gaps of 1.46 to 1.69 inside down and 1.65 to 1.81 between pairs, it never fell.
